# Norm of batch 0: low parts of K woven between the statistics, x's tiles in another queue, the root in PSUM

## The reference

```python
x = x + _L0_xattn_ref(_layernorm(x), ctx_4096, Wq, Wk, Wv, Wo)      # x: (4, 512, 1024)
x = x + _L0_ffn_ref(_layernorm(x), gate_w, up_w, down_w, fc1_w, fc2_w, expert_w, gamma, beta)
...
def _L0_xattn_ref(latents, context, Wq, Wk, Wv, Wo):
    hidden = jnp.concatenate([context, latents], axis=1)             # 64 rows of context, 512 of x
    q = (latents @ Wq.T)                                             # 16 heads of 96
    k = (hidden @ Wk.T)                                              # 4 heads of 96
    v = (hidden @ Wv.T)
    attn = softmax(q k / sqrt(96)); return (attn v) @ Wo.T
```

## Time and profile before

| | |
|---|---|
| time, median of 3 runs | 2171.95 us (2171.69 to 2172.54) |
| profiled execution, its own time | 2171.2 us |
| span of its instructions | 2169.3 us |
| PE busy | 2140.4 us (99%) |
| DVE, ACT, POOL busy | 769.4, 656.4, 698.6 us |
| the chain that ended last | PE 96% |

### The profile page before, as it was taken

The page is one execution under the profiler, slowest core; times in us unless marked ns, Lnnn a source line. Parts: engine busy times, 40 slices in busy tenths (PEclk is TensorE's granted clock), DMA queues, the critical chain, the costliest instruction groups (busy, mean ns, idle before and its releaser), DMA issues.

```text
span 2169.3 us, 30221 instructions
## 1 busy us (share of the span) xinstructions
PE 2140.4 (99%) x9884; PEld 1765.8 (81%) x9884; DVE 769.4 (35%) x1338; ACT 656.4 (30%) x1125; POOL 698.6 (32%) x560
## 2 busy tenths in 40 slices
PE   7999999999999999999999999999999999999998
PEld 6888888887778888878888878787887888888886
DVE  4223222167777777750100213222211142222222
ACT  4121111146666666661111223212123321111111
POOL 3500000136667677673212434100004422222221
PEclk9999999999999999999999999999999999999999
DMA  4732322525556555544433535312213532222222
GB/s 159 244 126 106 126 97 88 164 76 149 133 143 153 135 145 152 120 110 142 146 120 106 196 103 170 118 63 100 74 58 132 194 104 86 85 87 86 87 88 71
DMA packets 232525, 262.42 MB, mean 121 GB/s; under 512 B 78080, under 2 KB 145920, under 8 KB 232320
## 3 DMA queue, kind: packets, MB, share of 16 engines
q1 hardware_dynamic: 183888, 180.51, 26.7%
q10 hardware_dynamic: 48560, 80.95, 13.1%
HBM read 168.46 MB, written 92.67 MB: 120 GB/s over the span
## 4 chain that ended last, share of the span: by engine, by line
PE 96%; DMA 1%; DVE 1%; issue 1%; POOL 1%; ACT 1%; ACTq 0%; SPq 0%; DVEq 0%; POOLq 0%
PE psum L116 30%; PE psum L117 29%; PE psum L118 29%; PE psum L831 3%; PE psum L200 1%; PE psum L877 1%; PE psum L878 1%; DMA staging<-in_wqkv 0%; PE psum L1463 0%; PE psum L1462 0%; DMA recip_scratch<-small 0%; PE psum L838 0%; DMA staging<-in_ctx 0%; ACT operands L310 0%; DMA operands<-recip_scratch 0%
## 5 line engine op out<-in xcount | busy, mean ns | idle before, releaser
L116 PE MATMUL psum<-operands 128*128 128x512 f32 (+3 forms) x2952 | 1148.6, 389 | 12.5 <-DVE operands L315 6.9
L117 PE MATMUL psum<-operands 128*128 128x512 f32 (+3 forms) x2952 | 1137.3, 385 | 0.0
L118 PE MATMUL psum<-operands 128*128 128x512 f32 (+3 forms) x2952 | 1135.0, 384 | 0.0
L116 PEld LDWEIGHTS psum<-operands 128*128 128x128 f32 (+1 forms) x2952 | 556.7, 189 | 119.6 <-DVE operands L315 7.2
L118 PEld LDWEIGHTS psum<-operands 128*128 128x128 f32 (+1 forms) x2952 | 557.1, 189 | 108.9
L117 PEld LDWEIGHTS psum<-operands 128*128 128x128 f32 (+1 forms) x2952 | 558.3, 189 | 95.9
L762 POOL TENSOR_TENSOR operands<-staging,operands 128x512 fp32r<-128x512 f32 x192 | 247.9, 1294 | 165.6 <-ACT operands L922 165.5
L986 DVE TENSOR_REDUCE small<-psum 128x1 f32<-128x576 f32 x256 | 193.4, 755 | 138.9 <-PE psum L831 138.9
L1091 POOL TENSOR_TENSOR operands<-staging,operands 128x512 fp32r<-128x512 f32 x92 | 118.4, 1297 | 367.7 <-ACT operands L1086 367.1
L1690 POOL TENSOR_TENSOR operands<-operands 128x640 fp32r<-128x640 f32 x64 | 100.5, 1577 | 319.0 <-ACT operands L1685 318.8
L1542 DVE TENSOR_TENSOR staging<-staging 128x512 f32<-128x512 f32 x64 | 45.2, 726 | 304.7 <-ACT staging L1508 304.0
(11 more groups left out here) (89 smaller groups left out, 1129.2 us busy)
## 6 DMA issues: line engine op xcount, KB each, us to landing
h_scratch<-staging ACTq DMA_DIRECT2D x80, 256.0 KB, 2.1
operands<-h_scratch SPq DMA_DIRECT2D x64, 320.0 KB, 3.1
operands<-recip_scratch SPq DMA_DIRECT2D x64, 192.0 KB, 3.0
o_scratch<-staging SPq DMA_DIRECT2D x64, 192.0 KB, 3.3
operands<-o_scratch SPq DMA_DIRECT2D x64, 192.0 KB, 2.7
operands<-q_hi_scratch ACTq DMA_DIRECT2D x14, 768.0 KB, 6.2
operands<-q_lo_scratch ACTq DMA_DIRECT2D x14, 768.0 KB, 6.7
staging<-in_wqkv SPq DMA_DIRECT2D x36, 256.0 KB, 3.5
```

The lines of the kernel that those rows point to most:

```text
L116: e.matmul(o, lh, rh, start=first, stop=False)
L117: e.matmul(o, lh, rl, start=False, stop=False)
L118: return e.matmul(o, ll, rh, start=False, stop=last)
```

## The change

Three things are changed, all in p0. (1) VectorE makes the low parts of n = 6 to 9 as well, each behind the two statistics of one tile of x; GpSimd begins with n = 10, and TensorE waits for VectorE's semaphore where it waited for GpSimd's. (2) SyncE issues the four tiles of x, each ahead of one of the loads n = 6 to 9; ScalarE issues none. (3) For batch 0 ScalarE writes the root to PSUM (`rt_ps`). VectorE copies it to SBUF, which is one more operation, and refines it with operations that have at most one operand in SBUF. Later batches are as before.

```diff
+        rt_ps, nt_ps = PS[:, 7, 0:ST], PS[:, 7, 8:8 + ST]
...
                     for h in range(2):
                         link(e.bn_stats(stats[:, t, h, :], xn[:, t, h * NB:(h + 1) * NB]), (t, h) == (ST - 1, 1))
+                    if by_tile:
+                        by_tile(t)
...
-                link(e.tensor_tensor(nt1, rt, rt, ALU.mult))
-                link(e.tensor_tensor(nt1, nt1, ve, ALU.mult))
-                link(e.tensor_scalar(nt1, nt1, -0.5, 1.5, ALU.mult, ALU.add))
-                link(e.tensor_tensor(rstd, rt, nt1, ALU.mult))
+                if by_tile:
+                    e.tensor_copy(rt, rt_ps).then_inc(cp, 1)
+                    e.wait_ge(*past(cp, 1))
+                    e.sem_inc(idle, 1)
+                y, n1 = (rt_ps, nt_ps) if by_tile else (rt, nt1)
+                link(e.tensor_tensor(n1, y, rt if not by_tile else ve, ALU.mult))
+                link(e.tensor_tensor(n1, n1, ve if not by_tile else rt, ALU.mult))
+                link(e.tensor_scalar(n1, n1, -0.5, 1.5, ALU.mult, ALU.add))
+                link(e.tensor_tensor(rstd, n1, rt, ALU.mult))
...
-        BY_DVE, BY_POOL = list(range(6)), list(range(6, NF))
+        BY_DVE, BY_POOL = list(range(10)), list(range(10, NF))
...
         def p0_sp(e):
-            for n in range(NF + 6):
+            for n in range(10):
+                if n > 5:
+                    a_load_tile(e, x_r, n - 6)
+                raw_load(e, n)
+            for n in range(10, NF + 6):
                 raw_load(e, n)
...
                     if c and k % (DK // 2) == 0:
-                        e.wait_ge(*past(w_lop, 2 * c - 1 + k // (DK // 2)))
+                        e.wait_ge(*past(w_lod, 2 * c + 5 + k // (DK // 2)))
...
-            for n in range(5):
-                raw_high(e, n)
-            for t in range(ST):
-                a_load_tile(e, x_r, t)
-            for n in range(5, 13):
+            for n in range(13):
                 raw_high(e, n)
-            a_sqrt(e, 0)
+            a_sqrt(e, 0, rt_ps)
...
-            for n in BY_DVE:
+            for n in range(6):
                 raw_low(e, n, w_lod)
-            a_norm(e, 0, True)
+            a_norm(e, 0, lambda t: raw_low(e, 6 + t, w_lod))
```

More of the change, by code:

```diff
@@ L139, in norm_z @@
             sq = sem(f"{tag}_sqrt")
+            cp = sem(f"{tag}_sqrt_copied")
             zn = sem(f"{tag}_z")
@@ L154, in load_tile, with dve_norm @@
                 e.dma_start(xn[:, t, :], src[t * P:(t + 1) * P, :]).then_inc(ld_t[t], 16)
-            def dve_norm(e, b, by_tile=False):
+            def dve_norm(e, b, by_tile=None):
                 n = [0]
@@ L189, in dve_norm, with act_sqrt @@
                 z.then_inc(zn, 1)
-            def act_sqrt(e, b):
+            def act_sqrt(e, b, to=rt):
                 e.wait_ge(*past(ch, b * LN_CHAIN + 14))
-                e.activation(rt, rec, ACT.Sqrt).then_inc(sq, 1)
+                e.activation(to, rec, ACT.Sqrt).then_inc(sq, 1)
             def pe_t(e, b, k):
```

## The result

The changed kernel takes 2167.92 us (median of 17 runs, 2166.93 to 2170.96), the kernel before 2171.69 us on the same chips (17 runs, 2170.01 to 2173.68). The medians are 3.8 us apart; the ratio is 0.9984, 95% interval 0.9977 to 0.9991: 3.5 us less, between 2.0 and 5.0. The forecast was 2.6 us less, 2169.3 us, with 8 in 10 from 2167.2 to 2171.5.

What follows compares the result with a forecast made beforehand. TensorE, busy 2140.4 of 2169.3 us, bounds the kernel; only its waits can shrink, the last being for the fourth normalisation. Transposes at 28.85 instead of 31.47: 2171.95 - 2.6 = 2169.3 us, 8 in 10 from 2167.2 to 2171.5.

Steps and rivals of the forecast that it cites:

- what the transposes gain the program gains: In p0, the first transposes starting 2.6 us earlier (28.85 instead of 31.47) shortens the whole program by as much.
- The queue: Loads in p0: SyncE issues x 1.5 us earlier, the line moves at 398 GB/s, n = 10 lands at 17.6.
- rival D: Loads land no earlier (first form), or only by the 1.5 us of earlier issue (second): 2170.5 to 2172 us; chance 0.14.
- GpSimd's start sets the end: Norm of batch 0: ends at GpSimd's start, 18.3 (2.5 us earlier), + 7.48 + 2.98 = 28.8 us.
- The root in PSUM: Norm of batch 0: moves 3.3 us of small operations and gains nothing at the end.
- the two engines take turns: In the norm, 0.73 us of VectorE and 1.25 us of GpSimd alternate, to 28.8 for the last normalisation.
- A, VectorE keeps its turn: The four normalisations run back to back and end at 26.3: -4.5 us, 2167.4 us; chance 0.12.
- B, the clock: After TensorE's last rest before the transposes a second stretch is slow, 1.7 us of the gain go: 2171.0 us; chance 0.12.
- C: One queue does not fill the DMA engines: at 206 GB/s n = 10 lands 5.5 us later, 2177.4 us; chance 0.02.

Runs made afterwards that it cites:

- e3: The kernel before with only part 2, the tiles of x issued by SyncE ahead of the loads n = 6 to 9; ratio to before 0.9990.
- e4: The kernel before with only part 1, VectorE making the low parts of n = 6 to 9; ratio to before 0.9999.
- e1: The changed kernel with the root of batch 0 left in SBUF (part 3 undone); ratio to before 0.9988.
- e2: The kernel before with only part 3, the root of batch 0 in PSUM; ratio to before 0.9990.
- e5: The changed kernel, but GpSimd waits for the normalised x before the low part of n = 14; ratio to before 0.9974.
- e7: The changed kernel with x one place earlier in SyncE's queue and GpSimd waiting for the normalised x before n = 14; ratio to before 0.9975.
- e9: The changed kernel, but GpSimd waits for the normalised x already before n = 13; ratio to before 0.9973.
- e6: The changed kernel with each tile of x one place earlier in SyncE's queue; ratio to before 0.9986.

## Why the prediction was right

**That what the transposes gain the program gains** holds: stage a starts 11.5 to 11.6 us behind the end of the large operations in seven of the twelve kernels of the table; the others lie between 11.2 and 12.5, where the slow stretch of the clock lies otherwise or n = 15 is waited for.

**The queue** was right in kind and 0.5 us off in size. The prediction had n = 10 land at 17.6 from a line at 398 GB/s. Its high part starts at 18.16, or 3.41 MB in 9.2 us from 9.0: 371 GB/s on average. These are lines of the changed kernel, SyncE's first tile of x, then ScalarE's high parts of n = 6 and of n = 9 to 12, of which n = 10's is the second and starts at 18.16:

```profile
5.90 0.43 SPq L157 DMA_DIRECT2D staging<-in_x  x1
...
11.58 0.63 ACT L320 ACTIVATE operands<-staging 128x512 fp32r<-128x512 f32 x1 [1.77 <-DMA staging<-in_wqkv]
...
17.48 2.66 ACT L320 ACTIVATE operands<-staging 128x512 fp32r<-128x512 f32 x4 [1.33 <-DMA staging<-in_wqkv]
```

The average hides where the time went. From n = 6 to n = 10 the line moves three tiles and four halves, 2.62 MB, in 18.16 - 11.58 = 6.58 us, 398 GB/s as assumed; the shortfall lies ahead of that, where one tile and one half take from 9.17 to 11.58, 326 GB/s. Before, from n = 7 (high part at 14.30) to n = 10, it was 2.36 MB in 5.78 us, 408 GB/s, so the full line is no faster now; what is shorter is the stretch before it is full. The first tile is issued 1.67 us earlier (5.90 against 7.57) and n = 10's high part starts 1.92 us earlier (18.16 against 20.08). So the earlier issue, the second form of rival D, may account for most of what this part gives GpSimd; no run issues x earlier from ScalarE, and what the single line adds to it is not shown. The time that D gave, 2170.5 to 2172, is above the measured one all the same. e3 shows that this part alone brings x forward, e4 that part 1 alone brings nothing.

**That GpSimd's start sets the end** holds in e1, e2 and e4 too: from the start of the run to the end of the large ones it takes 10.63 us before, 10.64 in e1, 11.12 in e4 (with a held start), and 9.63 to 9.69 in the changed kernel and in e2, where the root is in PSUM.

**The root in PSUM** is the step whose size was off: "gains nothing at the end", with a sum that counted 2.98 us in full behind 7.48. It measured 0.84 us alone (e2) and 1.0 us on top of the rest (e1). What the runs show in its place is that a turn is cheaper than the two operations in a row. GpSimd's run grows by 8.36 - 7.48 = 0.88 us for the two large operations that come between, 0.44 each, and not 0.73. The 18.88 + 7.48 + 2.98 of the prediction's sum would be 29.34; measured is 28.51. The two errors, 0.6 us too early in the start and 0.8 us too late in the turns, nearly cancelled. That the end came out at 28.5 against 28.8 owes as much to this luck as to the sum; that the two engines take turns, and that most of the 3.3 us of the small operations is given back, was right.

The Trainium skill (SBUF — State Buffer, section Who interferes with whom) states both halves of this. It says that a VectorE instruction with at most one SBUF input outside the two-port modes does not contend with GpSimd; the trace agrees (0.16 to 0.17 us for five of them). It says that a `tensor_scalar` in a two-port mode contends with GpSimd, and that the one that comes second is fully blocked for the whole instruction of the other. The trace agrees that they hold each other, but not for the whole length: a turn costs GpSimd 0.44 us for an operation that occupies VectorE for 0.73, so about 0.3 us of it overlaps.

**The rivals.** A, VectorE keeps its turn, did not happen (one operation took 1762 ns). Much of what it would have been worth is gained in e5, 2.3 us on top of the change (1.5 without the clock's part). B, the clock, did not come true in the changed kernel. Before had two slow stretches, one over the first half of V, whose time is hidden, and one over the transposes; the changed kernel has only the second of them. Stretches of before, then of the changed kernel:

```profile
25.20:28.60 3.40, 3.17 (x11) 2.67 (x9) 2.95 (x4) 1.06 (x4) 3.07 (x3) 0.51 0.62 167
...
29.00:32.40 3.40, 3.40 (x18) 3.30 (x16) 2.15 (x4) 1.79 (x3) 0.00 (x0) 0.51 0.02 5
```

What B described is in e3 (0.9 us lost); e7 and e9 have no slow stretch at all up to stage a. C fell with the landings, as did D's first form.

The measured 3.5 us (2.0 to 5.0) agrees with stage a's 2.91 and with the forecast's 2.6 within the interval; where 0.6 us more would be from, if they are real, is not shown.

## What to carry to other kernels

When two engines exclude each other, moving small operations out of their way is worth less than their own time while large ones of the same kind stand behind them: 3.3 us of small operations gave 0.8 to 1.0 here, and the rest of the bill was paid by the large ones. Look for the work of the other engine that nobody needs yet and put it behind (e5: one wait, 1.5 us on top of the change, and 0.8 more by the clock), and stop where its own consumer starts to wait (e9). A transfer that is put ahead in a queue pushes back what an engine's order has in front of it (e6).

## What the runs showed of the hardware

Where the half-speed stretches of TensorE's clock fall differs between kernels that are the same up to that point; that it differs between executions of one kernel too is likely, for the mean granted clock of the changed kernel's runs lies between 0.995 and 0.998, but each kernel has one trace. Most lasted 3.4 us, one of e4 6.8 (from 15.2), the one of e3 10.2. They came behind a rest of TensorE or in one, but not with each: after a rest of 2.0 us and one of 1.2 us e9 had none, and e5, after the same 2.0 us, one. This one thing moved stage a by up to 0.9 us in a kernel whose other rows gained 1.5 (e3).

A `tensor_scalar` on 128x4 with a strided input waits for GpSimd as well (0.68 us at 19.52 in the changed kernel; 0.17 before at 22.03, where it met the end of a GpSimd operation); a `reciprocal`, `bn_stats` and `bn_aggr` did not (in the changed kernel 0.18 us for the reciprocal at 20.35 and 0.42 for the four `bn_aggr` at 18.94, in the midst of GpSimd's run; before 1.28 for the two `bn_stats` at 20.02, beside GpSimd's operation at 19.24).
